# Queries and keys of a differential attention, built on partitions by feature and fetched from DRAM

## The reference

```python
L1 = einsum(l2norm(q1), l2norm(k1)) * cos_scale      # (b, h, n, m)
L2 = einsum(l2norm(q2), l2norm(k2)) * cos_scale
G = tanh(delta_gain * (L1 - L2))                     # delta_gain: one per head
A1, A2 = softmax(L1 + G), softmax(L2 - G)
y = (A1 - lambda_full * A2) @ v
```

## Time and profile before

| | |
|---|---|
| median of 3 runs | 758.65 us (756.38 to 758.97) |
| the profiled execution | 760.07 us, span 758.3 us |
| TensorE busy | 664.0 us (88%) |
| VectorE busy | 553.7 us (73%) |
| ScalarE busy | 479.3 us (63%) |
| GpSimd busy | 247.4 us (33%) |
| mean granted TensorE clock | 0.975 |

### The profile page before, as it was taken

One profiled execution on the slowest core, in us unless ns is written; L12 is line 12 of the kernel. 1 busy time (PEld: TensorE's weight loads), 2 busy tenths in 40 slices (PEclk: granted clock), 3 DMA queues, 4 the chain that ended last, 5 costly groups with the idle time before them and its releaser, 6 DMA issues.

```text
span 758.3 us, 9794 instructions
## 1 busy us (share of the span) xinstructions
PE 664.0 (88%) x3514; PEld 287.7 (38%) x3514; DVE 553.7 (73%) x1058; ACT 479.3 (63%) x468; POOL 247.4 (33%) x394
## 2 busy tenths in 40 slices
PE   5999899999999888889988888798898787979795
PEld 2577545444454412222222222132232212547264
DVE  5656430605426389999999999999999997687656
ACT  1243433333342489999999999898999898213211
POOL 3601100102013745951378334547713030020001
PEclk9999999999999979999999999999999999989899
DMA  8000200000000111010111010110011130300430
GB/s 308 3 0 2 85 1 0 1 0 1 0 1 0 28 29 29 15 29 16 29 29 28 18 26 15 29 29 15 18 26 29 28 111 10 105 1 14 98 141 28
DMA packets 16752, 26.00 MB, mean 34 GB/s; under 512 B 2496, under 2 KB 7360, under 8 KB 16320
## 3 DMA queue, kind: packets, MB, share of 16 engines
q1 hardware_dynamic: 16704, 25.38, 12.1%
HBM read 15.87 MB, written 1.11 MB: 22 GB/s over the span
## 4 chain that ended last, share of the span: by engine, by line
PE 45%; ACT 22%; DVE 21%; issue 11%; POOL 1%; DMA 0%; POOLq 0%; DVEq 0%; ACTq 0%
ACT w_hh L881 17%; PE ps L590 7%; PE ps L600 7%; DVE hid L1144 5%; DVE hid L1149 5%; PE ps L630 4%; PE ps L538 4%; PE ps L577 4%; PE ps L519 3%; PE ps L639 3%; PE ps L618 2%; ACT probs L850 2%; PE ps L419 2%; PE ps L450 2%; PE ps L562 1%
## 5 line engine op out<-in xcount | busy, mean ns | idle before, releaser
L881 ACT ACTIVATE w_hh<-hid 128x2048 f32<-128x2048 f32 x128 | 249.0, 1945 | 13.2 <-DVE hid L1149 12.8
L519 PE MATMUL ps<-q_s,k_s 128*128 128x512 bf16 (+1 forms) x512 | 168.6, 393 | 25.6 <-DVE hid L1144 23.9
L538 PE MATMUL ps<-w_hh,v_h 128*32 128x512 f32 x1024 | 140.3, 620 | 31.1 <-ACT w_hh L881 28.6
L1149 DVE SCALAR_TENSOR_TENSOR hid<-ps,probs 128x1024 f32<-128x1024 f32 x86 | 104.6, 1217 | 6.5 <-PE ps L519 5.8
L1144 DVE TENSOR_TENSOR hid<-ps,probs 128x1024 f32<-128x1024 f32 x86 | 104.6, 1216 | 4.4 <-ACT w_hh L881 2.2
L519 PE MATMUL ps<-q_w,k_w 64*128 64x512 bf16 x256 | 100.4, 393 | 1.4 <-DVE hid L1149 1.1
L850 ACT ACTIVATE probs<-ps,gain 128x1024 f32<-128x1024 f32 x86 | 98.5, 1146 | 4.5 <-PE ps L519 4.3
L1479 POOL TENSOR_SCALAR rs<-mv 128x4 f32<-128x4 f32 x32 | 7.3, 227 | 249.6 <-DVE mv L960 249.4
L1053 DVE SCALAR_TENSOR_TENSOR hid<-ps,s_b,rot 128x512 f32<-128x512 f32 x16 | 11.9, 750 | 87.1 <-ACT rot L821 87.1
L519 PEld LDWEIGHTS ps<-q_s,k_s 128*128 128x128 bf16 (+1 forms) x512 | 38.4, 95 | 96.9 <-issue 47.3
L519 PEld LDWEIGHTS ps<-q_w,k_w 64*128 64x128 bf16 x256 | 23.6, 93 | 111.8 <-DVE hid L1149 65.0
(11 more groups left out here) (258 smaller groups left out, 1007.2 us busy)
## 6 DMA issues: line engine op xcount, KB each, us to landing
k_w<-k_s SPq DMA_DIRECT2D x32, 128.0 KB, 2.3
q_w<-q_s SPq DMA_DIRECT2D x32, 128.0 KB, 2.3
w_hh<-w_rows SPq DMA_DIRECT2D x4, 1024.0 KB, 9.0
w_hh<-in_b_h SPq DMA_DIRECT2D x2, 1024.0 KB, 8.8
hid<-w_rows SPq DMA_DIRECT2D x2, 1024.0 KB, 5.9
part<-w_rows SPq DMA_DIRECT2D x8, 256.0 KB, 7.0
x_res<-in_x SPq DMA_DIRECT2D x4, 256.0 KB, 6.0
tab<-in_rope SPq DMA_DIRECT2D x1, 1024.0 KB, 6.8
```

Of the source, the lines that this page charges most:

```text
L519: last = mm(ps[:, base + half, :], k_op[rows, u, keys], q_op[rows, u, half * CHUNK:(half + 1) * CHUNK], start=True, stop=True)
L538: last = mm(ps[VW * g4:VW * g4 + VW, 6, :], v_h[:, u, mt, :], ee[:, mt % 2, g4 * CHUNK:(g4 + 1) * CHUNK], start=(mt == 0), stop=(mt == BT ...
L881: A(ee[:, mt % 2, :], zz[:, mt % 2, :], ACT.Exp).then_inc(S["e"], 1)
L1149: v.scalar_tensor_tensor(zz[:, mt % 2, SEQ:2 * SEQ], banks[:, 4 * CHUNK:6 * CHUNK], -1.0, gg[s % 3], ALU.mult, ALU.subtract).then_inc(S["z ...
```

## The change

Queries and keys of C are projected with features on partitions (`c_raw`: 512 tokens wide) and values apart (`c_v`). The squares are summed over groups by products with a 0/1 matrix (`c_sums`), which puts the sums on tokens again; VectorE (chunks 0 and 1) or GpSimd (2 and 3) takes the roots and spreads the factors over 8 features (`spread`), TensorE transposes them (`c_scale`), and VectorE multiplies. The parts then are rows already. SyncE sends them to a DRAM tensor in six segments (`send`), and for each head loads ten blocks of 48 rows (`load_head`): each component of q and k twice, in its own and in the other half, and once the gained queries. These are queries times the head's `delta_gain`, made and split by GpSimd (`split_gained`, `send_g`), so that the difference product gives the argument of the tanh and `tanh_step` has no scale operand. `build_qk`, the turns of q and k, their copies and the crosswise copies go. Chunk 2's projection moves from the start of the C stage to turns at steps (0, 2) to (2, 3). SyncE sends chunk 2 before head 4's loads and chunk 3 before head 7's. A small exp ahead of the first tanh is new on ScalarE. GpSimd clears five operand tiles instead of two.

```diff
+SPECIAL = {(0, 2): ("raw", 0), (0, 5): ("raw", 1), (1, 1): ("v", 0), (1, 3): ("sums", 0), (2, 1): ("scale", 0),
+   (2, 3): ("scale", 1), (3, 1): ("late turn", 0), (3, 3): ("raw", 2), (3, 5): ("raw", 3), (3, 7): ("v", 1),
+   (4, 5): ("sums", 1), (5, 3): ("scale", 2), (5, 5): ("scale", 3),
+   (9, 7): ("y", 0), (10, 1): ("wo", 0), (10, 3): ("y", 1), (10, 5): ("wo", 1), (11, 5): ("x", 0),
    (12, 1): ("x", 1), (12, 3): ("route", 0), (12, 5): ("route", 1), (14, 6): ("w", 0)}
 def turning(n, mt):
...
-return ("q", n + 1)
-    if mt == 4:
-return ("o", n - 1) if n else None
+    if mt == 4 and n:
+return ("o", n - 1)
     return SPECIAL.get((n, mt))
-TURNS = [("k", 0), ("q", 0)] + [u for n in range(NH) for mt in range(BT) if (u := turning(n, mt))] + [("o", NH - 1)]
+TURNS = [u for n in range(NH) for mt in range(BT) if (u := turning(n, mt))] + [("o", NH - 1)]
...
+def spread(eng):
+    wide = [P, P, DH]
+    return eng.tensor_tensor(sq[:].rearrange("p a (n d) -> p (a n) d", d=DH),
+                             rstd[:].unsqueeze(2).to_broadcast(wide),
+                             cs_tab[:].rearrange("p a k h c -> p (a k h c)").unsqueeze(2).to_broadcast(wide), ALU.mult)
...
+    def send(c, i):
+        b, half = divmod(c, 2)
+        for a, order in enumerate((Q_PARTS, K_PARTS)):
+            for seg in range(PARTS):
+                if order[seg] == i:
+                    sp.dma_start(qk_rows[b, a, :, seg, :, half * CHUNK:(half + 1) * CHUNK],
+                                 part_of(i, c)[:, a, :]).then_inc(S["sent"], 16)
+    def send_g(c):
+        b, half = divmod(c, 2)
+        sp.wait_ge(S["glo_c"], c + 1)
+        for seg, i in enumerate(Q_PARTS):
+            sp.dma_start(qk_rows[b, 2, :, seg, :, half * CHUNK:(half + 1) * CHUNK],
+                         part_g[:, i, :]).then_inc(S["sent_g"], 16)
+    def load_head(n):
+        b, h = divmod(n, HEADS)
+        for comp in range(2):
+            at = HALF * comp
+            sp.dma_start(q_g[at:at + ROWS, n % 2, :],
+                         qk_rows[b, 2, 2 * h + comp].rearrange("s d t -> (s d) t")).then_inc(load[n % 2], 16)
+        for a, own, crossed in ((1, k_s, k_w), (0, q_s, q_w)):
+            for comp in range(2):
+                rows = qk_rows[b, a, 2 * h + comp].rearrange("s d t -> (s d) t")
+                for dst, at in ((own, HALF * comp), (crossed, HALF * (1 - comp))):
+                    sp.dma_start(dst[at:at + ROWS, n % 2, :], rows).then_inc(load[n % 2], 16)
+    for c in range(2):
+        sp.wait_ge(S["hi_c"], c + 1)
+        send(c, 0)
+        sp.wait_ge(S["mid_c"], c + 1)
+        send(c, 1)
+        sp.wait_ge(S["lo_c"], c + 1)
+        send(c, 2)
+        send_g(c)
+    sp.wait_ge(S["sent"], 2 * 16 * 2 * PARTS)
+    sp.wait_ge(S["sent_g"], 2 * 16 * PARTS)
+    sp.wait_ge(S["zeroed"], 1)
+    load_head(0)
+    load_head(1)
+    for n in range(2, NH):
+        if n in (4, HEADS - 1):
+            c = 2 if n == 4 else 3
+            sp.wait_ge(S["lo_c"], c + 1)
+            for i in range(3):
+                send(c, i)
+            send_g(c)
+        if n == HEADS:
+            sp.wait_ge(S["sent"], 4 * 16 * 2 * PARTS)
+            sp.wait_ge(S["sent_g"], 4 * 16 * PARTS)
+        sp.wait_ge(S["l2"], BT * (n - 1))
+        load_head(n)
...
-        if kind in "kq":
-            src, ready = (u_q, "uq") if kind == "q" else (u_k, "uk")
-            pe.wait_ge(S[ready], i + 1)
-            for j in range(BT):
-                last = nc.tensor.transpose(turn_bf[:, j * P:(j + 1) * P], src[:, i % 2, j, :], ident_bf[:])
...
-        elif kind == "late qkv":
-            last = mm(turn[:, 0:3 * P], xt_c[:, i * P:(i + 1) * P], w_c[:], start=True, stop=True)
+        elif kind == "raw":
+            if i == 0:
+                pe.wait_ge(S["xt_c"], CHUNKS - 1)
+            last = c_raw(i % 2, turn)
+        elif kind == "v":
+            last = c_v()
+        elif kind == "sums":
+            pe.wait_ge(S["sq_c"], CHUNKS - 1 + i)
+            last = c_sums(turn)
+        elif kind == "scale":
+            pe.wait_ge(S["fac_c"], CHUNKS - 1 + i // 2)
+            last = c_scale(i % 2, turn)
...
+        c_product(s, u, mt, 0, ((every, k_s, q_g), (every, k_s, q_g))).then_inc(S["dd"], 1)
...
+    def c_raw(a, bank):
+        return mm(bank, w_c[:, a * P:(a + 1) * P], xt_c[:], start=True, stop=True)
...
+    def c_sums(bank):
+        for a in range(2):
+            for k in range(CT):
+                o = (a * CT + k) * GROUPS
+                last = mm(bank[:, o:o + GROUPS], sq[:, a, k * P:(k + 1) * P], grp, start=True, stop=True)
+        return last
+    def c_scale(a, bank):
+        for k in range(CT):
+            last = nc.tensor.transpose(bank[:, k * P:(k + 1) * P], sq[:, a, k * P:(k + 1) * P], ident[:])
+        return last
...
-        for k in range(CT):
-            if CT * c + k >= 2:
-                pe.wait_ge(S["vraw_c"], CT * c + k - 1)
-            mm(ps[:, 5 + k % 2, 0:3 * P], xt_c[:, k * P:(k + 1) * P], w_c[:],
-               start=True, stop=True).then_inc(S["qkv_c"], 1)
+        if c:
+            pe.wait_ge(S["qh_c"], c)
+        for a in range(2):
+            c_raw(a, ps[:, 5 + a, :]).then_inc(S["qkv_c"], 1)
+        c_v().then_inc(S["qkv_c"], 1)
...
+            if c >= 2 and o == 1:
+                pe.wait_ge(S["fac_c"], c - 1)
+                for a in range(2):
+                    last = c_scale(a, ps[:, 5 + a, :])
+                last.then_inc(S["f_c"], 1)
...
-            if c == CHUNKS - 1 and o == 2:
-                c_turning(("k", 0))
...
-        if c == CHUNKS - 1:
-            c_turning(("q", 0))
...
+        if 1 <= c < CHUNKS - 1:
+            pe.wait_ge(S["sq_c"], c)
+            c_sums(ps[:, 5, :]).then_inc(S["sums_c"], 1)
...
+    pe.wait_ge(load[0], 16 * LOADS)
     c_diff(0, 0, 0)
-    pe.wait_ge(S["crossed"], 64)
     c_first(0, 0, 0)
-    c_prep(CHUNKS - 2)
+    pe.wait_ge(S["yo_b"], CHUNKS)
+    c_second(0, 0, 0)
     c_diff(1, 0, 1)
-    pe.wait_ge(S["yo_b"], CHUNKS)
-    pe.wait_ge(S["vraw_c"], TILES - CT)
-    c_second(0, 0, 0)
     c_first(1, 0, 1)
     c_second(1, 0, 1)
     c_diff(2, 0, 2)
...
-                    pe.wait_ge(S["turn_read"], turns_done(("q", n3)))
+                    pe.wait_ge(load[n3 % 2], 16 * LOADS * (n3 // 2 + 1))
...
-        A(gg[s % 3], banks[:, 0:2 * CHUNK], ACT.Tanh, scale=gain[:, u:u + 1]).then_inc(S["g"], 1)
+        A(gg[s % 3], banks[:, 0:2 * CHUNK], ACT.Tanh).then_inc(S["g"], 1)
...
-    act.wait_ge(S["gcp"], 1)
+    me.mark(A(tiny[:, 56:57], tiny[:, 0:1], ACT.Exp))
     tanh_step(0, 0, 0)
-    c_evac_qkv(CHUNKS - 2)
     tanh_step(1, 0, 1)
...
+    def c_norms(c):
+        dve.wait_ge(S["sums_c"], c + 1)
+        me.step(v.tensor_scalar(nv[:], ps[:, 5, 0:P], 1e-12, 1e38, ALU.max, ALU.min))
         rsqrt_start(rstd[:], whole)
-    def c_factor():
-        return v.tensor_tensor(rstd[:], rstd[:], cs_tab[:].rearrange("p a h k c -> p (a h k c)"), ALU.mult)
-    def c_norms(c):
-        c_sums(c)
         for _ in range(3):
             rsqrt_newton(rstd[:], whole)
-        me.step(c_factor())
-        v.tensor_tensor(sq[:].rearrange(groups, d=DH), raw[:].rearrange(groups, d=DH),
-                        rstd[:].unsqueeze(2).to_broadcast([P, P, DH]), ALU.mult).then_inc(S["qh_c"], 1)
+        spread(v).then_inc(S["fac_c"], 1)
+    def c_high(c):
+        dve.wait_ge(S["f_c"], c + 1)
+        v.tensor_tensor(sq[:].rearrange("p a t -> p (a t)"), raw[:].rearrange("p a t -> p (a t)"),
+                        banks[:, 5 * CHUNK:7 * CHUNK], ALU.mult).then_inc(S["qh_c"], 1)
...
+        if c == 1:
+            c_table(dve, v, me)
+        if c >= 2:
+            c_norms(c - 2)
         if c:
             add_out("b_out", c - 1, y[:])
         if c + 1 < CHUNKS:
             dve.wait_ge(S["tp_b"], c + 1)
             apply("b_in", c + 1, x_of(c + 1), xn[:], "xn_b")
+        if c >= 2:
+            c_high(c - 2)
         if c == 0:
             c_const()
         else:
             c_in(c - 1)
-        if c == 1:
-            c_table(dve, v, me)
         if c >= 2:
-            c_norms(c - 2)
+            c_middle(c - 2)
+            c_low(c - 2)
         if c:
             c_apply(c - 1)
...
-        if kind == "k":
-            last = v.tensor_copy(k_s[:, i % 2, :], turn_bf)
-        elif kind == "q":
-            last = v.tensor_copy(q_s[:, i % 2, :], turn_bf)
...
+        elif kind == "raw":
+            dve.wait_ge(S["lo_c"], CHUNKS - 2 + i // 2)
+            last = v.tensor_copy(raw[:, i % 2, :], turn)
+        elif kind == "v":
+            last = v.tensor_copy(v_of(CHUNKS - 2 + i), turn.rearrange("p (t h v) -> p t h v", t=CT, h=HEADS))
+        elif kind == "sums":
+            last = v.tensor_scalar(nv[:], turn[:, 0:P], 1e-12, 1e38, ALU.max, ALU.min)
+        elif kind == "scale":
+            last = v.tensor_tensor(sq[:, i % 2, :], raw[:, i % 2, :], turn, ALU.mult)
...
+            if use and use[0] == "sums":
+                dve.wait_ge(S["turn_read"], turns_done(use))
```

(52 more changed lines are left out.)

## The result

| | before | after |
|---|---|---|
| median | 757.51 us (756.27 to 758.97, 4 runs) | 764.75 us (761.95 to 764.83, 4 runs) |
| the profiled execution, its span | 760.07, 758.3 | 764.83, 763.0 |
| mean granted TensorE clock in it | 0.975 | 0.973 |

The ratio is 1.0085, with an interval of 1.007 to 1.010: slower by 7.2 us by the medians. The forecast was 760.2, with 0.36 on "same" and 0.34 on "slower"; by the prediction's own line of 0.5% the result is on the slower side. Of the 7.2, 4.8 are between the two profiled executions, which is what I can place; the rest is that the profiled execution of before (760.07) lay above all of its timed runs.

A forecast was written before the change was run, and what follows sets the result against it. ScalarE's exp and tanh were taken to bound the C stage, TensorE the B stage. Terms -9.4 -4.2 +8.3 -3.5 -1.5 +3.2 +8.6 = +1.5 gave 761.6 us profiled, 760.2 as a median; range 749 to 776.

The forecast's parts named there:

- A: Rival, faster: SyncE's queue is quick, 0.46 per issue and 6.7 for the gain; 753 us, chance 0.26.
- D: Rival, faster: the stalls at heads 4 and 7 do not exist, GpSimd's split being misplaced; 748 us, chance 0.06.
- Step 1: C stage, ScalarE: tanh without scale operand saves 0.09 us in some 104 of 127 intervals; -9.4 us.
- Step 2: C stage, VectorE: two copies per head leave, saving in heads 9, 10, 11, 13 and 14; -4.2 us.
- Step 3: B stage, TensorE: new sums, transposes, and stalls of 2.6 and 1.4 for the factors; +8.3 us.
- Step 4: Start of C stage: first product to first exp shortens, -3.5 us; the first head's excess falls, -1.5 us.
- Step 5: SyncE's queue: chunks 2 and 3 sent ahead of loads stall heads 4 and 7, +3.2 and +8.6 us.
- B: Rival, slower: each store or load takes SyncE, or the DMA engines behind it, 1 us; 779 us, chance 0.18.
- C: Rival, slower: the scale operand's 90 ns hide in the overlap of two activations; 770 us, chance 0.12.

The follow-up runs named there:

- e6_before_noscale: The kernel before with the tanh's scale operand left out (delta_gain not applied): 750.58 us, ratio 0.9907.
- e5_scaled: e4_both with the tanh given a scale operand again, a column of ones: 753.12 us, ratio 0.9942.
- e4_both: The changed kernel with the edits of e1_order and e3_later together: 746.15 us, ratio 0.985.
- e7_copies: e4_both with two extra VectorE operations per head, at the steps where k and q were copied: 754.05 us, ratio 0.9954.
- e3_later: The changed kernel with the factors' transposes and ScalarE's splitting copies one output of the hidden layer later: 759.53 us, ratio 1.0028.
- e1_order: The changed kernel with SyncE sending chunk 2 before head 5's loads and chunk 3 before head 8's, one head later each: 749.29 us, ratio 0.989.

## Why the prediction came out as it did
The mechanisms were there, each in its place. The forecast was 4.5 us below the median. In the profile the sum was 3 us short: the holes by 3.8 and the B stage by 2.0, with less than the forecast at the start of C (0.5), in the D stage (1.5) and in the steps of the C stage (0.4). The other 1.3 come from the carried-over difference between the profiled execution and the median: 1.4 for before, 0.1 for after. The prediction also gave "faster" 0.30, though A and D, both faster, have 0.32 between them.

- **Step 1, the tanh** (-9.4): it measured -7.3 in e6_before_noscale. The 90 ns were right (0.905 from start to start, step 2.705). The count of 104 intervals was too large: 7.3 / 0.09 is 81 with the copies in place, and the 8.2 of e5_scaled make 91 without them.
- **Step 2, the copies** (-4.2, with a bound of -5): underestimated. e4_both is the C stage of the change without holes: 358.90 against 374.42, so -15.5. Of this -7.3 is the tanh (e6_before_noscale, of which 1.0 in the first head), and the first head gives 1.9 more (24.88 to 23.02). The other heads, where the copies' going is the main difference, give -6.4. e7_copies, which puts such work back, costs 7.6. Steps 1, 2 and the first head summed to -15.1 in the forecast and to -15.5 in the runs: two errors that cancel, which is luck.
- **Step 3, the B stage** (+8.3, measured +10.3). The stalls were forecast at 2.6 and 1.4 and are 2.44 and 1.27; the transposes took 0.93 from start to start, against 1.1. What this step had wrong is that a stall was priced at its idle time: the low clock behind the first adds 1.9 (e4_both), nearly the whole miss of 2.0. The prediction had such a low clock only in the upper tail of its chances, not in the sum. What else was off cancels: stalls and transposes 0.6 less, the sums and projections of two chunks 0.4 more (+1.5 each, not +1.3).
- **Step 4, the start of C** (-3.5, measured -4.0): right. The first head gives back 3.3 instead of 1.5, a part of it the tanh's.
- **Step 5, the queue.** Head 4's chain counted from head 2's first exp, forecast and measured: split starts 11, 11.7; split ends 21.2, 21.8; gains end 29.0, 29.0; last store issued 32.3, 33.3; last load issued 37.8, 38.1; product 39.6, 40.1. The hole is 3.37 for 3.2 forecast. But the head lost 6.2, since the steps behind the hole ran at half the clock (e3_later, with the same hole at full clock, lost 3.5). Head 7's hole is 8.84 for 8.6, and its head lost 9.4. So this step lacks 3.8 of 15.6, nearly all behind the holes, not in them. Its issue time, 0.55 for all, is 0.64 for stores and 0.47 for loads: behind the gains that makes 6 x 0.64 + 10 x 0.47 = 8.5 where 8.8 was forecast. Head 0's last load was issued at 261.12; with 2.5 to landing that leaves 2.2 us until 265.86, where 3 was forecast, and e4_both shows the wait once TensorE is there 6.0 earlier.
- **D stage** (0, measured -1.5): VectorE's and ScalarE's busy time there is the same (78.96 and 79.00, 28.19 both), the granted clock went from 0.93 to 0.94. I put it down to that.

**The rivals.** A (753, quick queue): its loads were quick (0.47) but not its stores, and its gain chain of 6.7 was 7.2. B (779, 1 us per issue): ruled out by 0.64 and 0.47. C (770, the operand's time hidden): ruled out by e5_scaled and e6_before_noscale. D (748, no stalls): wrong in this kernel, but close to what e1_order gives once its cause is taken away. The Trainium skill (DMA: Bandwidth & Descriptors, section Anatomy of one DMA, written for DMAs that GpSimd issues) calls the receipt of a write heaviest where the target is HBM. It did not show in these stores, which SyncE issues, either:
```profile
qk_rows<-part SPq DMA_DIRECT2D x48, 128.0 KB, 2.3
...
qk_rows<-part_g SPq DMA_DIRECT2D x24, 128.0 KB, 2.3
q_g<-qk_rows SPq DMA_DIRECT2D x32, 96.0 KB, 2.2
...
q_w<-qk_rows SPq DMA_DIRECT2D x32, 96.0 KB, 2.5
```
2.3 us from issue to landing in DRAM is what the copy inside SBUF took in the earlier trace rows.

So the change is a gain of 15.5 us in the C stage and 4.0 at its start, against 10.3 in the B stage and 15.6 in two holes that one line of SyncE's order makes. What stays open: why the medians differ by 7.2 and the profiled executions by only 4.8. The runs of one kernel differ by as much (after's fastest, 761.95, is 2.8 below its median), but no profile shows where before's other runs are shorter.

## What to carry to other kernels
A queue that serves two purposes is an order of due times: before a batch is put into it, ask what stands behind it and when that is needed; here moving 36 stores behind the loads of the next head was worth 15.5 us with not one instruction saved. Price a stall on TensorE at its length, and keep a second price for the work behind it at half the clock; here 2.4 and 3.4 us of idle time cost 4.3 and 6.2, but 3.4 in another execution 3.5, and 8.8 cost 9.4. And when the bounding engine gets faster, work on the next engine that was hidden before is hidden less: count it at the new rate.

## What the runs showed of the hardware that was not expected
- **The clock after idle time is no function of its length alone.** After 2.44 us of idle it fell to 0.54 for some 4 us, after 1.27 it did not fall (behind both came eight transposes, 0.93, before the next products), after 3.37 it fell to 0.50 in one execution, and after 3.40 at the same place in another it did not. In the hole of 8.84 it was at 0.50 from 428 on, in the hole itself, and at 1.00 again from 438 on.
- **GpSimd and VectorE slow each other on operands in SBUF.** With VectorE idle, GpSimd's second split of the gained queries took 1.49 (248.48). Earlier in the B stage, beside VectorE's 1024-column subtraction of two SBUF tiles, both were longer, GpSimd 2.34 and VectorE 2.06 (1.22 for the subtraction at 196.12). Timelines of GpSimd and VectorE in after:
```profile
200.02 2.34 POOL L1610 TENSOR_SCALAR part_g<-g_q 128x512 bf16<-128x512 f32 x1
```
```profile
198.95 2.06 DVE L1200 TENSOR_TENSOR part<-raw,part 128x1024 bf16<-128x1024 f32 x1 [1.60 <-ACT part L905]
```
  They look as if they took turns: GpSimd's operation before ended at 199.94, and 1.22 from there is 201.16, where VectorE ended at 201.01; 1.49 from that end is 202.50, where GpSimd ended at 202.36. Beside the z operations, which read one operand from PSUM, GpSimd's split took 1.49 as well (342.96). The Trainium skill, GPSIMD Engine Reference, section Key points, tells of contention with VectorE instructions that have two inputs in SBUF; the trace agrees.
- **SyncE's issue time is not the same for all transfers:** 0.64 for a store of 128 partitions into rows of a DRAM tensor, 0.47 for a load of 48 whole rows. The direction alone does not make it: the four loads into 128 partitions in the earlier trace rows took 0.62 each.
